# A recurrent kernel on one core: relay queues, filler products, key products and the first recurrent piece rearranged

## What is computed

```
def rec_step(carry, inp):
    R, h = carry
    zt, kt, vt, bt = inp
    q_rec = softmax(h)
    v_old = einsum('bhij,bhj->bhi', R, kt)
    R = R + (bt * (vt - v_old))[..., :, None] * kt[..., None, :]
    h = zt + einsum('bhij,bhj->bhi', R, q_rec)
    return ((R, h), h)
```

## Time and profile before

| what | us |
|---|---|
| median of 3 runs | 689.8 (689.74 to 691.82) |
| the profiled execution | 690.92 |
| its span, first to last instruction | 689.2 |
| relay of the coefficients | 214 to 268 |
| recurrent steps 0 to 15 | 268 to 458 |
| PE, DVE, ACT, POOL busy | 589.3, 425.8, 354.7, 346.5 |

### The profile page before, as it was taken

The page is one execution under the profiler, slowest core; times in us unless marked ns, Lnnn a source line. Parts: engine busy times, 40 slices in busy tenths (PEclk is TensorE's granted clock), DMA queues, the critical chain, the costliest instruction groups (busy, mean ns, idle before and its releaser), DMA issues.

```text
span 689.2 us, 12546 instructions
## 1 busy us (share of the span) xinstructions
PE 589.3 (86%) x4570; PEld 462.9 (67%) x4570; DVE 425.8 (62%) x1097; ACT 354.7 (51%) x910; POOL 346.5 (50%) x459
## 2 busy tenths in 40 slices
PE   6879999998997762688888799969997789899996
PEld 3637777777555652577777688756786668775776
DVE  3643653415766777979998699983144755654534
ACT  0064454453996662145677687405423555666440
POOL 1597562303802763898999998415454100001335
PEclk9999999999999995679999999999999899998998
DMA  7000000000000433000000000000000000000000
GB/s 258 3 1 1 1 0 1 1 1 1 0 1 22 78 76 93 5 0 2 1 1 1 0 1 2 1 1 1 1 1 1 2 1 2 1 1 1 9 9 16
DMA packets 10701, 10.38 MB, mean 15 GB/s; under 512 B 5904, under 2 KB 9680, under 8 KB 10384
## 3 DMA queue, kind: packets, MB, share of 16 engines
q1 hardware_dynamic: 7936, 7.54, 3.9%
q0 software_dynamic: 1984, 1.62, 1.1%
q10 hardware_dynamic: 720, 0.41, 0.2%
HBM read 5.70 MB, written 0.52 MB: 9 GB/s over the span
## 4 chain that ended last, share of the span: by engine, by line
PE 57%; DVE 12%; POOL 11%; ACT 8%; issue 4%; DMA 4%; SPq 3%; ACTq 0%; POOLq 0%; DVEq 0%
PE bank L1187 8%; PE bank L1175 8%; PE bank L1452 4%; PE bank L1490 4%; PE bank L1264 4%; PE bank L1488 4%; POOL features L555 3%; SPq L428 3%; DVE bank L1911 3%; PE bank L1536 2%; PE bank L1224 2%; DVE features L1905 2%; PE bank L1524 2%; PE bank L1233 2%; POOL coefs L414 2%
## 5 line engine op out<-in xcount | busy, mean ns | idle before, releaser
L1264 PE MATMUL bank<-ident,features 128*128 128x128 f32 x604 | 84.9, 296 | 17.5 <-DVE features L1881 16.7
L1264 PEld LDWEIGHTS bank<-ident,features 128*128 128x128 f32 x604 | 75.3, 155 | 24.5 <-DVE features L1881 23.2
L798 ACT ACTIVATE G<-bank,cols 128x512 f32<-128x512 f32 x64 | 43.5, 687 | 52.1 <-PE bank L1175 52.1
L1175 PE MATMUL bank<-xs,weights 128*128 128x512 f32 x128 | 59.5, 609 | 4.6 <-ACT xs L789 4.6
L555 POOL TENSOR_TENSOR features<-UV,coefs 128x1024 f32<-128x1024 f32 (+3 forms) x36 | 59.4, 1669 | 4.6 <-DVE UV L1868 4.6
L1187 PE MATMUL bank<-weights,G 128*128 128x128 f32 x512 | 59.8, 275 | 0.0
L1187 PEld LDWEIGHTS bank<-weights,G 128*128 128x128 f32 x512 | 58.4, 192 | 0.0
L372 POOL TENSOR_SCALAR rstd<-mv 128x4 f32<-128x4 f32 x8 | 1.9, 236 | 108.6 <-DVE mv L384 108.6
L1881 DVE TENSOR_TENSOR features<-UV,bank 128x1024 f32<-128x1024 f32 (+3 forms) x68 | 55.7, 863 | 1.2 <-PE bank L1264 0.3
L880 ACT ACTIVATE xs<-UV,coefs 128x32 f32<-128x32 f32 x216 | 47.0, 308 | 0.0
L1911 DVE TENSOR_REDUCE bank<-features 128x32 f32<-128x1024 f32 (+3 forms) x40 | 41.1, 1054 | 3.6 <-POOL features L574 3.6
(11 more groups left out here) (336 smaller groups left out, 1438.5 us busy)
## 6 DMA issues: line engine op xcount, KB each, us to landing
weights<-in_w SPq DMA_DIRECT2D x2, 1024.0 KB, 11.4
features<-in_tok SPq DMA_DIRECT2D x1, 768.0 KB, 5.8
weights<-in_ew SPq DMA_DIRECT2D x4, 128.0 KB, 3.1
weights<-in_ew SPq DMA_DIRECT2D x2, 256.0 KB, 2.9
coefs<-G SPq DMA_DIRECT2D x16, 25.5 KB, 3.7
rows<-in_rows SPq DMA_DIRECT2D x1, 384.0 KB, 6.9
out_h<-H SPq DMA_DIRECT2D x3, 128.0 KB, 2.0
coefs<-G POOLq DMA_DIRECT2D x14, 25.5 KB, 3.4
```

The costliest lines, as they stand in the source:

```text
L798: act.activation(G[:, 4 * (w % 2) + f, :], up_bank(f)[:], ACT.Gelu, bias=col("b1", 4 * i + f)).then_inc(s["tok_gelu"], 1)
L1175: mm(up_bank(f)[:], w1[:, i, P * f:P * f + P], xT[:, w % 2, :], start=True, stop=True).then_inc(s["tok_up"], 1)
L1264: last = mm(out[:, P * k:P * k + P], x[:, P * k:P * k + P], ident[:], is_transpose=True, start=first and k == 0, stop=last_ and k == n - 1 ...
```

## The change

1. The relay DMAs of a group are split 3 (SP) and 5 (POOL), in every fourth group 4 and 4 (`from_sync`).
2. The multiplication of the position table moves from DVE to POOL, behind POOL's relays; DVE works out the gate's part before the sum of the table. PE issues 28 products whose result nobody reads ahead of the table's turns, and 10 behind them.
3. Row strengths are computed four rows at a time, behind `next_query` of steps 0, 2 and 3, where rows 8 to 15 were done behind step 1. POOL's waits for them move (t = 2, 4, 5), and its `weigh_keys` of rows 8 to 15 is split over t = 4 and 5.
4. `warm(6)` and its wait begin at t = 2.
5. POOL makes a second key piece (j = 2) from t = 14. `key_products(t - 1)` moves forward in POOL's stream: into `held(t)` at t = 12 and 13 (ahead of the piece that starts at row 4 and row 8), ahead of `queries` at t = 15.
6. From step 6 on (7 rows and more) the recurrent products start with a piece of two rows, then fours.

The name `full` becomes `wide` in one loop, with no effect.

```diff
 def last_row_alone(n):
-    return pieces(n - 1) + [(n - 1, n)] if n > 1 else [(0, 1)]
+    if n < 7:
+        return pieces(n - 1) + [(n - 1, n)] if n > 1 else [(0, 1)]
+    return [(0, 2)] + [(r + 2, e + 2) for r, e in pieces(n - 3)] + [(n - 1, n)]
...
 KEYS = 10
+KEYS2 = 14
+
+def keys_until(t):
+    return max(0, t - KEYS) + max(0, t - KEYS2)
+
+def key_pieces(t):
+    return [j for j, lo in ((1, KEYS), (2, KEYS2)) if t >= lo]
...
+        def from_sync(g):
+            return 4 if g % 4 == 1 else 3
+
         def relay(eng, g, j):
...
-                .then_inc(s["coef_%d" % (g % NS) if j < 4 else "copy_last" if g == NG - 1 and j > 5 else "copy_%d" % (g % NS)], 16)
+                .then_inc(s["coef_%d" % (g % NS) if j < from_sync(g) else
+                            "copy_last" if g == NG - 1 and j > 5 else "copy_%d" % (g % NS)], 16)
...
-                for j in range(0, 4):
+                for j in range(from_sync(g)):
                     relay(sp, g, j)
...
                 for i, r0, r1_ in helds_of(t):
                     R = r1_ - r0
+                    if t in (12, 13) and r0 == CH * (t - 11):
+                        key_products(t - 1)
...
                 if t >= KEYS:
                     pool.wait_ge(s["h_exp"], exps_of(t + 1))
-                    pool.tensor_tensor(PD[:, 1, :].rearrange("p (r x) -> p r x", r=CH), RK[:, CH:2 * CH, :],
+                for j in key_pieces(t):
+                    pool.tensor_tensor(PD[:, j, :].rearrange("p (r x) -> p r x", r=CH), RK[:, CH * j:CH * j + CH, :],
                                        expS[:].unsqueeze(1).broadcast_to([P, CH, HB]), ALU.mult).then_inc(s["key_p"], 1)
...
-                for j in range(4, 6 if g == NG - 1 else GB):
+                for j in range(from_sync(g), 6 if g == NG - 1 else GB):
                     relay(pool, g, j)
 
+            pool.wait_ge(s["p_done"], 1)
+            pool.tensor_tensor(plog, plog, comb[:, 0, 24:32].unsqueeze(2).broadcast_to(full), ALU.mult)\
+                .then_inc(s["p_done"], 1)
...
-                     4: (("rows", 8, 16), ("less", 8, (11, 10))),
-                     5: (("less", 8, (9, 8, 7)),),
+                     4: (("rows", 8, 12), ("less", 8, (11, 10))),
+                     5: (("less", 8, (9, 8, 7)), ("rows", 12, 16)),
...
                 held(t)
+                if t == T - 1:
+                    key_products(t - 1)
                 queries(t)
-                key_products(t - 1)
-                if t < CH:
-                    pool.wait_ge(s["query_scaled" if t == 1 else "sums_done"], max(1, t))
+                if t not in (12, 13, T - 1):
+                    key_products(t - 1)
+                if t == 1:
+                    pool.wait_ge(s["query_scaled"], 1)
+                if t in (2, 4, 5):
+                    pool.wait_ge(s["sums_done"], 2 if t == 2 else t - 1)
...
-            pe.wait_ge(s["p_done"], 1)
+            for k in range(28):
+                mm(held_sum[:, HB:2 * HB], ident[:], RK[:, 0, :], start=True, stop=True)
+            pe.wait_ge(s["p_done"], 2)
...
                 last.then_inc(s["p_T"], 1)
+            for k in range(10):
+                mm(held_sum[:, HB:2 * HB], ident[:], RK[:, 0, :], start=True, stop=True)
...
-                if t >= CH:
+                if t >= 2:
                     pe.wait_ge(s["o_add"], t)
                     warm(6)
...
+            def row_strengths(c):
+                r = slice(CH * c, CH * c + CH)
+                normalisers(r)
+                ch.settle()
+                strengths(r)
...
-                mine = [j for j in range(len(cuts)) if j != 1 or t < KEYS]
+                mine = [j for j in range(len(cuts)) if j not in key_pieces(t)]
...
-                if t >= KEYS:
-                    dve.wait_ge(s["key_p"], t - KEYS + 1)
-                    summed(1)
+                for n, j in enumerate(key_pieces(t)):
+                    dve.wait_ge(s["key_p"], keys_until(t) + n + 1)
+                    summed(j)
...
                 if t == 0:
-                    normalisers(slice(CH, 2 * CH))
-                    ch.settle()
-                    strengths(slice(CH, 2 * CH))
+                    row_strengths(1)
                 if t + 1 < T:
                     next_query(t + 1)
-                if t == 1:
-                    normalisers(slice(2 * CH, T))
-                    ch.settle()
-                    strengths(slice(2 * CH, T))
+                if t in (2, 3):
+                    row_strengths(t)
...
-                ch(dve.tensor_tensor(f, f, share, ALU.mult))
+                dve.tensor_tensor(f, f, share, ALU.mult).then_inc(s["p_done"], 1)
                 ch(dve.tensor_tensor(gate[:, 3, :], gate[:, 2, :], share, ALU.mult))
-                ch.settle()
-                dve.tensor_tensor(plog, plog, f.unsqueeze(2).broadcast_to([P, NH, P]), ALU.mult).then_inc(s["p_done"], 1)
```

20 lines of the change are left out of this document (12 added, 8 removed).

## The result

| | kernel before | changed kernel |
|---|---|---|
| median, first series (4 runs each) | 690.81 us | 703.33 us (702.18 to 703.80) |
| ratio, 95% interval | | 1.0163 (1.0122 to 1.0204) |
| median, second series (25 and 4 runs) | 690.92 us | 696.87 us |
| ratio, 95% interval | | 1.0101 (1.0043 to 1.0159) |
| span of the profiled execution, first series | 689.2 us | 700.4 us |

The change makes the kernel slower, by 12.5 us in the first series and 6.0 in the second (medians). The forecast was 682.4 us, 7.4 faster. Medians are of all executions, ratios leave out those over 1.5% above the fastest of their kernel, so that the two need not agree; by the ratios it is 11.3 and 7.0 us.

What follows compares the result with a forecast made beforehand. No engine is busy throughout; chains that differ by stage set the end. Gains and losses from step 0 to step 15 summed to 7.4 us off the 689.8 us median, giving 682.4; range 680.4 to 686.6.

Steps and rivals of the forecast that it cites:

- (a): Relay split: with issue as the limit, copies end near 253.6 instead of 257.6, last relay lands near 262.7 instead of 268.03.
- (b): Fillers and table ahead of step 0: PE free at 271.1, `query_sub(1)` at 273.8, gain 1.8 us.
- (c): Row strengths in pieces, steps 1 to 3: `query_sub(2)` at 279.3, gain 3.35; then gains of 3.05 and 3.15 us.
- (d): `warm(6)` in steps 2 and 3: 2.6 us each, hidden under DVE's 1.27; step 4 loses its slow PE stretch, gain 4.3.
- (g): Key products earlier at t = 12 and 13: +2.1 us at step 11, then -0.35 and -0.65 at steps 12 and 13.
- first rival: DMA engines or landings hold the relay, so it is not faster: copies end at 257.6, time 686.4 us; chance 0.15.
- rival 3: Fillers ahead of step 0 run at 1.2 GHz, PE free 17.5 us later: 699.9 us; chance 0.04.
- (e): POOL's solve split, 1.08 us of `weigh_keys` moved to t = 5: product at 316.96 starts at 313.2, gain 3.75.
- (f): Two rows first from step 6: +0.4 us in all at full clock, value near nothing.
- Rival 2: POOL's added work holds the steps, and keys ahead of held pieces delay `turn_held`: 684.6 us; chance 0.14.
- (h): Second POOL key piece, steps 14 and 15: +0.9 and +1.3 us in the sum.
- Behind the loop: The code after the last step, 231 us, taken as untouched and starting from the last step's state.

Runs made afterwards that it cites:

- b2_split: Kernel before with the relay DMAs split three on SP and five on POOL (four and four in every fourth group), nothing else: 690.54 us, ratio 1.0004.
- b4_sp5: Kernel before with five relay DMAs of a group on SP, three on POOL (four and four in every fourth group and the last): 697.44 us, ratio 1.0076.
- b3_fill: Kernel before with the 28 and 10 filler products around the position table's turns, nothing else: 694.75 us, ratio 1.0067.
- a1_split44: Changed kernel with its relay DMAs split four and four again: 695.39 us, ratio 1.0074.
- c3_psum: c1_best with VectorE's first row-strength product of rows 8 to 11 taking an operand from PSUM instead of SBUF: 688.96 us, ratio 0.9973.
- c5_key2: Kernel before with the second POOL key piece from step 14 and, at step 15, key products ahead of the queries: 689.59 us, ratio 0.9974.
- c6_both_psum: c3_psum with the second row-strength product of rows 8 to 11 also taking its first operand from PSUM: 690.13 us, ratio 0.9990.
- b1_two: Kernel before with the recurrent piece of two rows alone: 689.62 us, ratio 0.9994.
- c1_best: Changed kernel with relay four and four, no 38 fillers, recurrent pieces in fours, key products of steps 12 and 13 late: 690.14 us, ratio 0.9985.
- c8_key2_warm13: c5_key2 with 13 instead of 6 filler products ahead of step 15's recurrent products: 690.11 us, ratio 0.9955.

## Why the prediction was wrong

Three kinds of steps failed. The relay brought none of the 4 us that were booked for it, since landings grew while I held them fixed (a). The fillers' cost stood in the sum at nothing (b). And the gains of steps 1 to 4 and of step 11 were reckoned against falls of the clock in one execution of the kernel before (c, d, g).

(a) *The relay.* The step that failed first. I took the issue as the limit, from 28% busy DMA engines, and let the copies end at 253.6; they ended at 260.87. POOL's issue time was right (0.487 us each). What I left fixed was the way to landing, "3.5 to 4.5 us": it became 5.7 in the median, for SP's DMAs as for POOL's. Relays took 44.0 us on average where four and four takes 43.0 and I forecast 38: no gain where I booked 4 us. My first rival said this, with 0.15. (In SP's sum the long issues left over are 48.0 - 40.6 - 1.0 = 6.4 us and not 7; it changes nothing, since POOL's queue was the slower one.) The rule that I weighed there (the Trainium skill, DMA: Bandwidth & Descriptors, Issuing engines are not separate DMA queues: more issuers save only issue time) came nearer than my sum: by it the split gives nothing, and b2_split measured 1.0004. Its general form isn't borne out here, since with five on SP the issue time did cost (b4_sp5, 1.0076).

(b) *Fillers.* The size was right: 17.6 us from the copies' end to a free TensorE, `query_sub(1)` 20.2 us behind the copies (forecast 273.8 - 253.6), and 21.7 or 21.8 where the clock was low in the fillers. The conclusion wasn't. It held only if the copies ended 4 us earlier, so the fillers' cost stood in the sum at nothing; without fillers `query_sub(1)` follows the copies by 14.9 to 19.4 us. I had written that the fillers "set step 0", and asked what they cost only if they ran at 1.2 GHz (rival 3). They cost 4.6 us in b3_fill, in whose profile all but their first 3.2 us ran at 2.4 GHz.

(c), (d) *Strengths in pieces, `warm(6)` in steps 2 and 3.* Steps 1 to 4 took 31.5 us, forecast 30.4: step 1 took 6.1 for 5.5 (the clock fell in it; 5.51 in a1_split44, where it didn't) and step 2 8.6 for 7.7. The wait for POOL's product is a term that I didn't have; by itself it makes step 2 1.1 us longer in c3_psum, and in this profile the clock would have made it as long without it. The larger error is in what I set these steps against. The 32.9 us of the kernel before hold two long falls of the clock, 17.1 us each; the same code takes 29.6 (c5_key2) and 29.9 us (b2_split, b3_fill) where less of them lies in these steps. I booked 3 us of one execution's clock as a gain of the change. `warm(6)` hides as forecast, unless the clock is low (the first profile, c6_both_psum).

(e) *Solve.* Step 5 takes 9.56 us with it and without it. No gain.

(f) *Two rows.* Forecast +0.16, +0.16, -0.10 at steps 6, 7 and 8, -0.09 and +0.17 at steps 13 and 14; measured +0.16, +0.15, -0.10, -0.09, +0.17 (b1_two against the kernel before; step 13 15.18 for 15.27). In these five steps the formula of arrival and rows left holds to 0.01 us. It has no term for step 11 (twelve rows), and in steps 12 (-0.24 for 0) and 15 (+0.28 for +0.17) the clock's falls are mixed in.

(g) *Early key products.* Forecast +2.1 at step 11, then -1.0 at 12 and 13. The second part came (0.9), the first didn't: steps 10 and 11 took 30.4 to 32.4 us with them (seven profiles, mean 31.4) and 29.1 to 32.8 without (twelve, mean 30.8). POOL's part was right: from the start of the key product to the end of the held pieces 6.3 us forecast, 6.2 measured. Right too is the length of step 11 at full clock, 16.2 us forecast (18.26 - 2.1), 16.17 in a1_split44. In the first profile it took 18.6, since I had let TensorE run "at full clock to 388.7" and it did not. But the gain was again reckoned against a fall: step 11 of the kernel before took 18.26 us with TensorE at 1.2 GHz at its end, and steps 10 and 11 together took 31.8, where they take 29.5 in c1_best without a fall in either and 29.5 in b2_split and b3_fill with one in step 10. Rival 2 named the delay ("keys ahead of held pieces delay `turn_held`").

(h) *Second key piece.* Forecast 0.9 and 1.3; measured 1.1 and 0.7 (c5_key2). Right in the sum.

*Behind the loop.* I took its 231 us as fixed. They were 228.3 to 236.3 us, by the time that the clock was low there, and 5.8 us of the first profile's loss are of this kind.

Added up, the single costs are 4.6 (fillers) + 1.0 (relay, by means) + 0.5 to 1.5 (strengths: the changed steps 1 to 4 took 31.3 on average of eight profiles; the old ones 30.9 in seven, 29.8 in the three fastest of them) + 0.3 (two rows) + 0.9 (early keys, steps 12 and 13) - 1.8 (second key piece) = 5.5 to 6.5 us, beside 6.0 (medians) or 7.0 (ratio) measured in the second series. The fillers and the second key piece are measured in kernels of their own. The strengths are not, the relay's 1.0 us is within its scatter, and b2_split shows none of it. So the sum is plausible, not shown.

It also leaves out what comes behind the loop: 234.4 us on average in the seven profiles of the changed kernel and its variants, 230.9 in the six of the kernel before and its variants (b and c5_key2), but 228.3 to 235.4 in c1_best and its three variants, and 234.1 in c8_key2_warm13. Whether the change makes falls of the clock more frequent there, and whether part of the loss is of this kind, is open.

## What to carry to other kernels

Take a baseline for a step from several profiles, or from rows without a fall of the clock, before a change is credited with it. Filler products in the queue of an engine are paid in full if what stands behind them would have been ready: compare their end with the arrival of the real work, not with the idle that they fill. A VectorE product with both inputs in SBUF can be held until a GpSimd product beside it ends (1.38 us for 0.22 here), so place it where none is under way.

## What the hardware showed that I had not expected

- With five of eight relay DMAs issued by GpSimd the DMA engines were 51% busy from 218 to 262 us (changed kernel), with four 33% (a1_split44), at 73 and 75 GB/s; the median landing was 5.7 us and 4.3, and SP's DMAs were as late as GpSimd's.
- A VectorE product of 128x64 took 0.22 us or up to 1.73 us (a1_split44), by whether a GpSimd product that reads SBUF was under way and where its inputs lay.
- The same code behind the loop took 228.3 us with 17.7 us of it at the lower clock level and 236.2 with 35.7 us; filling one idle time of 3.3 us moved the nearest falls and left the later ones.
